# Attention and 4-bit feed-forward layer on one core: the quantised levels are transposed by SyncE's DMA queue instead of by TensorE

## The reference

```python
h = layernorm(x)
Q, K, V = h @ Wq.T + bq, h @ Wk.T + bk, h @ Wv.T + bv          # 16 heads of 32
scores = Q K^T / sqrt(32) - (i - j), causal                     # softmax over j
x = x + layernorm(attn(V) @ Wo.T + bo)
xh = layernorm(x) @ hadamard
scale = max|xh| over the row / 7
q = clip(round(xh / scale), -8, 7)                              # the levels
x = x + layernorm((q * scale) @ ternary(weight).T)
```

## Time and profile before

| | |
|---|---|
| time, median of 3 runs | 1174.39 us (1171.98 to 1174.9) |
| profiled execution | 1171.96 us, span 1170.3 us |
| busy | PE 1095.2 us (94%), DVE 988.7 (84%), ACT 707.8 (60%), POOL 588.0 (50%) |
| chain that ended last | PE 72%, DVE 18%, issue 4%, DMA 3% |
| mean granted TensorE clock | 0.968 of full speed |

### The profile page before, as it was taken

The page is one execution under the profiler, slowest core; times in us unless marked ns, Lnnn a source line. Parts: engine busy times, 40 slices in busy tenths (PEclk is TensorE's granted clock), DMA queues, the critical chain, the costliest instruction groups (busy, mean ns, idle before and its releaser), DMA issues.

```text
span 1170.3 us, 44847 instructions
## 1 busy us (share of the span) xinstructions
PE 1095.2 (94%) x18656; PEld 732.9 (63%) x18656; DVE 988.7 (84%) x2562; ACT 707.8 (60%) x1493; POOL 588.0 (50%) x715
## 2 busy tenths in 40 slices
PE   4899999999999999999999999999999999998652
PEld 3566666676666666766666666666666676665321
DVE  5748998889988888899988888898888889987574
ACT  5445666766666667666666666656666666565432
POOL 2334555555555555555545555555555565454411
PEclk9989999999999999999999999999999999999765
DMA  9746667755657676656566676556667665554231
GB/s 272 159 87 139 140 155 160 163 138 139 139 119 138 155 164 164 139 132 136 127 139 153 165 159 138 127 123 139 151 152 165 148 151 133 116 113 120 65 64 47
DMA packets 204831, 161.81 MB, mean 138 GB/s; under 512 B 150448, under 2 KB 150704, under 8 KB 204528
## 3 DMA queue, kind: packets, MB, share of 16 engines
q1 hardware_dynamic: 199888, 141.86, 55.7%
q0 software_dynamic: 4736, 17.04, 4.1%
HBM read 40.87 MB, written 16.78 MB: 49 GB/s over the span
## 4 chain that ended last, share of the span: by engine, by line
PE 72%; DVE 18%; issue 4%; DMA 3%; SPq 2%; ACT 1%; POOLq 1%; POOL 0%; DVEq 0%; ACTq 0%
PE f_job L1356 46%; PE f_st L1457 5%; PE f_o L1474 5%; PE f_o L1479 4%; PE f_job L1533 3%; PE f_job L1432 2%; PE f_job L1515 2%; DVE f_stage L955 2%; DVE f_bst L1001 2%; DVE f_rmax L969 2%; PE f_job L1523 1%; DVE f_inverse L993 1%; DVE f_x L1045 1%; DVE f_o L991 1%; PE f_job L1440 1%
## 5 line engine op out<-in xcount | busy, mean ns | idle before, releaser
L488 POOL TENSOR_SCALAR_AFFINE_SELECT f_PT<-f_PT 64x512 f32<-64x512 f32 (+1 forms) x256 | 203.4, 812 | 157.6 <-ACT f_PT L654 107.5
L503 POOL TENSOR_TENSOR f_square<-f_stage 128x512 bf16<-128x512 f16 x128 | 131.1, 1047 | 92.1 <-ACT f_stage L632 79.3
L494 POOL TENSOR_TENSOR f_OTl<-f_o,f_OTh 128x256 f16<-128x256 f32 x127 | 84.6, 673 | 140.0 <-ACT f_OTh L672 140.0
L1356 PE MATMUL f_job<-f_xTh,f_wqh 128*128 128x256 f16 x512 | 140.8, 275 | 14.9 <-DMA f_xTl<-f_xl 14.8
L632 ACT ACTIVATE f_stage<-f_job,f_bias 128x256 f16<-128x256 f32 x256 | 106.6, 468 | 75.9 <-PE f_job L1356 68.7
L1356 PE MATMUL f_job<-f_xTh,f_wql 128*128 128x256 f16 x512 | 140.2, 274 | 0.0
L1356 PE MATMUL f_job<-f_xTl,f_wqh 128*128 128x256 f16 x512 | 140.1, 274 | 0.0
L1356 PE MATMUL f_job<-f_xTh,f_wkl 128*128 128x256 f16 x512 | 139.7, 273 | 0.0
L1356 PE MATMUL f_job<-f_xTh,f_wkh 128*128 128x256 f16 x512 | 139.7, 273 | 0.0
L1356 PE MATMUL f_job<-f_xTl,f_wkh 128*128 128x256 f16 x512 | 139.7, 273 | 0.0
L955 DVE SCALAR_TENSOR_TENSOR f_stage<-f_job,f_bias,f_stage 128x256 f16<-128x256 f32 x256 | 110.9, 475 | 32.7 <-ACT f_stage L632 32.7
(11 more groups left out here) (197 smaller groups left out, 2975.9 us busy)
## 6 DMA issues: line engine op xcount, KB each, us to landing
f_stacks<-f_stage SPq DMA_DIRECT2D x380, 128.0 KB
f_xin<-x SPq DMA_DIRECT2D x32, 512.0 KB, 6.2
f_x<-x SPq DMA_DIRECT2D x32, 512.0 KB, 4.5
out<-f_z POOLq DMA_DIRECT2D x31, 512.0 KB, 3.5
f_Vmix<-f_V SPq DMA_DIRECT2D x32, 256.0 KB, 6.2
f_Vmix<-f_V SPq DMA_DIRECT2D x64, 128.0 KB, 6.3
f_stacks<-rows_const SPq DMA_DIRECT2D x3, 512.0 KB, 4.9
f_stacks<-wqT SPq DMA_DIRECT2D x2, 512.0 KB, 5.8
```

The lines of the kernel that those rows point to most:

```text
L488: nc.gpsimd.affine_select(out=d, in_=d, compare_op=ALU.is_ge, fill=0.0, base=odd * SUB, pattern=[[0, 4], [0, TP], [1, SUB]], channel_multi ...
L494: nc.gpsimd.tensor_tensor(OT[s % 2][1][:, g, :], o32[:, g % 2, :], OT[s % 2][0][:, g, :], ALU.subtract).then_inc(OTl_made, 1)
L503: nc.gpsimd.tensor_tensor(square[:, 2 * m + pair, :], h, h, ALU.mult).then_inc(squared, 1)
L1356: mm = pe.matmul(dst, lhs[a](c), rhs[b](c), start=(n == 0), stop=(n == 3 * KC - 1))
```

## The change

For the first 29 steps of levels (`k < by_queue = STEPS - 3`) `turn_q` and `keep_q` are gone. SyncE issues one transposing transfer of `q16[:, t, :]` straight into `qT[:, t]` for each tile (`turn_levels`), and `second` and `x2_high` wait for its semaphore. The last three steps keep the path over TensorE, PSUM and ScalarE. In SyncE's loop `mix_values` stands ahead of `load_res`, `load_front` stands behind `turn_x`, and the two `turn_levels` stand among the restacking transfers.

```diff
+        q_moved = [sem(f"q_moved{t}") for t in range(TP)]
...
+        by_queue = STEPS - 3
+
+        def levels_read(k, t):
+
+            return (q_moved[t], 16 * (k + 1)) if k < by_queue else (q_turned, TP * (k - by_queue) + t + 1)
...
+            def turn_levels(k, t):
+
+                sp.wait_ge(q_made, TP * k + t + 1)
+                until(sp, f_product, TP * (k - 1) + t + 1)
+                sp.dma_start(qT[:, t], q16[:, t, :], transpose=True).then_inc(q_moved[t], 16)
...
+                if s:
+                    mix_values(s)
                 if has(k):
                     load_res(k)
+                restack_high(n)
+                if has(k - 1):
+                    turn_levels(k - 1, 0)
+                restack_low(n, (0, 1))
+                if has(k - 1):
+                    turn_levels(k - 1, 1)
+                restack_low(n, (2, 3))
+                if has(m):
+                    turn_x(m)
                 if has(m + 1):
                     load_front(m + 1)
-                if s:
-                    mix_values(s)
-                restack_high(n)
-                restack_low(n, range(4))
-                if has(m):
-                    turn_x(m)
                 if has(k):
                     turn_x2(k, 0)
                     turn_x2(k, 1)
...
             def x2_high(k, t):
                 act.wait_ge(folded, 2 * (TP * k + t) + 2)
-                until(act, q_turned, TP * (k - 1) + t + 1)
+                if k:
+                    act.wait_ge(*levels_read(k - 1, t))
...
                 if has(k - 1):
                     round_levels(k - 1, 1)
-                    keep_q(k - 1, 0)
...
                 invert(s, 0)
-                if has(k - 1):
-                    keep_q(k - 1, 1)
                 invert(s, 1)
...
             def second(k, t):
                 claim("f", t, k)
...
-                pe.wait_ge(qT_made, TP * k + t + 1)
+                if k < by_queue:
+                    pe.wait_ge(q_moved[t], 16 * (k + 1))
+                else:
+                    pe.wait_ge(qT_made, TP * (k - by_queue) + t + 1)
...
                     out_product(k, 0)
-                if has(k - 1):
-                    turn_q(k - 1, 0)
...
                 if has(k - 1):
-                    turn_q(k - 1, 1)
                     second(k - 1, 0)
```

More of the change, by code:

```diff
@@ L689, in keep_q @@
             def keep_q(k, t):
-                act.wait_ge(q_turned, TP * k + t + 1)
+                act.wait_ge(*levels_read(k, t))
                 until(act, f_product, TP * (k - 1) + t + 1)
@@ L1368, in _ @@
                        "h": lambda k, t: (q_made, TP * k + t + 1),
-                       "q": lambda k, t: (qT_made, TP * k + t + 1), "f": lambda k, t: (z_made, TP * k + t + 1)}
+                       "q": lambda k, t: (qT_made, TP * (k - by_queue) + t + 1), "f": lambda k, t: (z_made, TP * k + t + 1)}
             def claim(kind, i, step):
```

## The result

| | before | after |
|---|---|---|
| median of 4 runs | 1173.39 us | 1192.51 us (1189.28 to 1194.60) |
| ratio, 95% interval | | 1.0162 [1.0146, 1.0179] |
| profiled execution, span | 1170.3 us | 1189.2 us |
| granted clock, mean of the span | 0.97 | 0.97 |

The change makes the kernel 1.6% slower, by 19 us. The forecast was 1166.8 us, with 1160 to 1177 as its range.

What follows compares the result with a forecast made beforehand. A TensorE-then-VectorE loop of 33.10 us was taken to set usual steps, TensorE alone those beginning a sequence. Savings of 22 x 0.22 and 7 x 0.40, together 7.6 us, gave 1166.8 us, range 1160 to 1177.

Steps and rivals of the forecast that it cites:

- the two `keep_q`: ScalarE copies of 0.6 us each, outside its chain before front_high; removing them was called worth nothing and unable to cost.
- VectorE's 26.74 us: Gapless VectorE stretch from y_out(k, 1) to the step's end, part of the 33.10 us loop that sets the pace.
- rival 1: VectorE's stretch hides slack, so TensorE's whole saving is won: 11.6 to 16.0 us, 1158.4 to 1162.8; chance 0.17.
- The restacking: SyncE's last piece lands between 434.1 and 434.7, scores(n, 0) asks at 434.7: margin 0 to 0.6 us, no loss.
- the small DMA share from 431.5 us: Share of 0.10, read as restacking done 1.9 us after its last issue began; landing put at most at 2.5.
- Rival 2: Late restacking makes TensorE wait in 15 steps, 4.5 us back, 1171.3 us, no measurable change; chance 0.20.
- the two `turn_q`: TensorE transposes of 0.22 and 0.18 us: removal saves 0.22 in a usual step, 0.40 in one beginning a sequence.
- The limit on the other side: TensorE's own loop falls to 32.55 us, below the 32.88 us pace, so its waits for VectorE grow.
- The moved loads: SyncE's load_front behind turn_x and mix_values ahead of load_res: all at nothing, covered by SyncE's 9.5 us of waiting.
- The levels of tile 1: Their transfer lands before the second `second` asks at 432.9: margin 1.4 us by the median, -1.0 by the maximum.
- rival 4: Levels land late, `second` waits 1.0 us in 22 steps: 7 us slower, 1181.5; chance 0.05.
- rival 3: SyncE's transposing issues stretch to 2.5 us, restacking lands late: 16 to 25 us slower, about 1190 to 1200; chance 0.10.

Runs made afterwards that it cites:

- keep_later: Kernel before with one ScalarE line moved: keep_q of tile 1 behind the exponentials of head group 2 instead of ahead; 1194.9 us, ratio 1.0174.
- no_transfer_filled: Changed kernel without the levels' transfers (second reads a constant tile), with three unused ScalarE copies where keep_q stood; 1164.4 us, ratio 0.9912 to the kernel before.
- order_only: Kernel before with only SyncE's loads reordered: mix_values ahead of load_res, load_front behind turn_x; 1173.0 us, ratio 0.9988.

## Why the prediction was wrong

*The step that failed* is the one on the two `keep_q`: "Worth nothing; as its cover was never needed it can't cost." ScalarE had the time, but the instruction behind the waiting `keep_q` was `exps(s, 2, 0)`, which releases GpSimd's masks together with the exponentials after it, and their start decides who is stretched beside VectorE's gapless stretch. I asked whom the removed wait delayed and not what it kept apart. Measured: +0.93 us in a usual step (keep_later), 16 to 22 us in all. The prediction held every number needed but one: it called VectorE's 26.74 us gapless, and it named in rival 1 that an instruction there "can be longer than it need be, beside GpSimd's". It took this for a possible gain only. GpSimd's row of 2.71 us where the pair before it took 1.37 was the sign, and it was not read.

*The restacking* was given a margin ("0 to 0.6 us") and "I take no loss". The place was right, waits of `scores` for `f_stacks`. The issue time was right too (1.25 us, forecast 1.27), and so was the landing of the last piece by its median, 2.5 us, but not by the reading that gave it. The prediction took the small DMA share from 431.5 us on the earlier trace rows for the end of restacking, 1.9 us after the last issue; the landing events of that trace put it at 433.4, 3.7 us after. What was mis-sized is the place and the spread: the last piece was issued 11.5 us after the mark by the median, 12.8 at most, where the sum had 11.2, and it took up to 3.9 us to land, where the sum had at most 2.5. The forecast was a landing 13.1 to 13.7 us after the mark; it came at 12.9 to 15.8, later than 13.7 in 18 of 29 steps, and TensorE waited in 14. Cost: 13.5 us without the clash, 7.7 in the changed kernel. Rival 2 had this place and a giveback of 4.5 us, by a landing 0.6 us longer in each of 15 steps; the waits that came were up to 2.2 us long.

*What held.* Removing the two `turn_q` brings 0.22 us in a usual step and 0.40 or a little more in the others: 32.88 us in no_transfer_filled, to the hundredth, and 34.25 for the first of a sequence (forecast 34.3). The limit on the other side held too: TensorE's own work in that step is 32.57 us (forecast 32.55), and it waits for VectorE in 19 steps. Between profiled executions 7.4 us were won against 7.6 forecast; between medians 10.3, with an interval of 8.5 to 12.3 us. The traced execution of before, 1171.96 us, lies 2.7 below the median of 1174.67 that the 10.3 counts from; its slower executions were not traced, so why the medians differ by more stays open. The moved loads cost nothing (order_only was 1.7 us faster). The levels of tile 1 were late only 3 times, 1.6 us in all, with 1.4 us of margin by the median: rival 4 did not happen.

*The rivals.* The time fell into rival 3's band, 1190 to 1200 us, but not by its mechanism, so that is luck: the transposing issues mostly did not stretch (median 1.25 us, 9 of 58 over 1.4, 2.70 at most), and 12.6 of the 18.6 us came from VectorE and GpSimd, which no rival had.

The net is: a gain of 7.6 us forecast and 10.3 measured; the clash takes 21.8, the transfers 13.5, and the overlap of the two gives 21.8 - 16.0 = 5.8 back. -10.3 + 21.8 + 13.5 - 5.8 = 19.2, against 19.1 measured. That the sum closes is no proof, since the four terms come from the same four kernels; the proof is in the steps and in keep_later.

## What to carry to other kernels

When a change takes out a wait off the critical path, look at what the waiting engine does next and which third engine that releases: the wait may be what keeps two engines out of each other's way. An instruction on an engine with idle time that lasts twice as long as its like (2.71 us beside 1.37) can mark such a meeting; here the busy engine beside it was a shift of 0.85 us away from paying itself. And a margin worked out from medians, in a queue whose issues stretch (2.65 us to 3.70 for the four high pieces), has to be held against the longest row: half of a change (one transfer instead of two) may keep the gain and fit.

## What the runs showed of the hardware

- A GpSimd masking pair of 64x512 and VectorE's instructions with two SBUF operands stretched each other when they met. Which of them is stretched depends here on where they meet: GpSimd by 1.34 us when it arrives 5.61 us after `y_out(k, 1)`, VectorE by 2 x 0.46 us when it arrives 4.76 us after it. In the first case GpSimd did not get in between any of VectorE's six instructions that follow each other without a gap; in the second it did, ahead of a small one (L1063) and of L1069. Why it gets in at one seam and not at another, no run here shows.
- ScalarE is 60% busy before. Three useless copies a step put into the changed kernel made it 16 us faster, and moving one copy behind two exponentials in the kernel before made that 20 us slower.
- A 128x512 transpose issued between restacking transfers landed in 3.3 us by the median and 5.1 at most, where the same shape in the earlier trace rows has 2.5 and 4.9.
